# Where the residual's beta is added: a GpSimd addition moved from the scan stage to the coupling stage, with two swaps in ScalarE's order

## What is computed

```python
x = layernorm(x + coupling(x))                 # x2, the residual tokens of the next layer
xz = x @ w_in.T + b_in;  x_ssm, z = split(xz);  z = silu(z)
dt = softplus(x_ssm @ w_dt.T + b_dt)
Bm, Cm = x_ssm @ w_B.T + b_B, x_ssm @ w_C.T + b_C
h_n = exp(A_n * dt) * h_n + dt * Bm_n * x_ssm  # along the sequence, 16 states n
y = sum_n(h_n * Cm_n) + D * x_ssm
pre = (y * z) @ w_out.T + b_out + x            # residual: x is x2
attn = (pre - mean) * rsqrt(var + eps) * gamma + beta
x = layernorm(x + attn)                        # x2 + beta + gamma * normalized
```

## Time and profile before

| | |
|---|---|
| median of three runs | 1106.31 us (1105.72 to 1107.59) |
| the profiled execution: its own time | 1105.93 us |
| its span, first to last instruction | 1104.1 us |
| TensorE matmul busy | 991.2 us (90%) |
| VectorE busy | 935.2 us (85%) |
| ScalarE busy | 850.1 us (77%) |
| GpSimd busy | 720.8 us (65%) |
| DMA, mean share of 16 engines | 45.5% |
| mean granted TensorE clock | 0.970 |

### The profile page before, as it was taken

One profiled execution on the slowest core, in us unless ns is written; L12 is line 12 of the kernel. 1 busy time (PEld: TensorE's weight loads), 2 busy tenths in 40 slices (PEclk: granted clock), 3 DMA queues, 4 the chain that ended last, 5 costly groups with the idle time before them and its releaser, 6 DMA issues. The chain is left out here.

```text
span 1104.1 us, 17792 instructions
## 1 busy us (share of the span) xinstructions
PE 991.2 (90%) x5502; PEld 742.3 (67%) x5502; DVE 935.2 (85%) x1232; ACT 850.1 (77%) x1664; POOL 720.8 (65%) x623
## 2 busy tenths in 40 slices
PE   6999999999969999998758699999999999988887
PEld 4777777777755555555546477767777777777776
DVE  7999999999955888865889998999999999999851
ACT  7778878877646677777767798898988989887843
POOL 3466566756760112215878998989989898999630
PEclk9999999999998999999878899999999999999899
DMA  6444434443415001114967675456665558665201
GB/s 187 128 134 120 134 102 139 121 121 104 120 30 192 1 29 49 39 57 107 247 142 188 129 169 134 138 148 140 173 147 161 150 135 171 146 148 141 78 11 39
DMA packets 93249, 133.86 MB, mean 121 GB/s; under 512 B 8802, under 2 KB 47714, under 8 KB 93156
## 3 DMA queue, kind: packets, MB, share of 16 engines
q1 hardware_dynamic: 93156, 132.73, 45.5%
HBM read 116.45 MB, written 14.16 MB: 118 GB/s over the span
## 5 line engine op out<-in xcount | busy, mean ns | idle before, releaser
L2325 DVE TENSOR_TENSOR_SCAN ob<-bank_a,h,ob 128x512 f32<-128x512 f32 x128 | 159.7, 1269 | 15.6 <-ACT bank_a L1992 13.4
L2325 DVE TENSOR_TENSOR_SCAN oa<-bank_a,h,oa 128x512 f32<-128x512 f32 x128 | 160.5, 1271 | 12.7 <-ACT h L2001 6.7
L1804 PE MATMUL bank_m<-w,f_h 128*128 128x256 f32 x448 | 104.5, 383 | 0.0
L1481 POOL TENSOR_TENSOR oa<-ob,x1T 128x1024 f32<-128x1024 f32 x8 | 18.8, 2354 | 129.9 <-DVE ob L1381 129.9
L1992 ACT ACTIVATE bank_a<-s,A 128x512 f32<-128x512 f32 x128 | 86.6, 684 | 17.7 <-DVE ob L2325 13.6
L1992 ACT ACTIVATE bank_a<-dtc,A 128x512 f32<-128x512 f32 x128 | 86.7, 684 | 15.5 <-DVE ob L2325 10.0
L1804 PEld LDWEIGHTS bank_m<-w,f_h 128*128 128x128 f32 x448 | 84.7, 193 | 13.0 <-issue 2.4
L1749 PE MATMUL bank_y<-ident,ob 128*128 128x128 f32 x512 | 71.6, 286 | 19.2 <-POOL ob L2558 13.3
L883 POOL TENSOR_TENSOR xd<-xs,L 128x512 f32<-128x512 f32 x32 | 33.9, 1060 | 76.0 <-DVE xs L662 76.0
L1749 PEld LDWEIGHTS bank_y<-ident,ob 128*128 128x128 f32 x512 | 63.2, 148 | 29.6 <-POOL ob L2558 14.2
L673 DVE TENSOR_TENSOR_SCAN L<-abc,zeros,b_id 128x512 f32<-128x512 f32 x64 | 78.3, 1265 | 5.2 <-POOL xd L883 4.2
(11 more groups left out here) (407 smaller groups left out, 2944.3 us busy)
## 6 DMA issues: line engine op xcount, KB each, us to landing
Bb<-CB_rows SPq DMA_DIRECT2D x128, 256.0 KB, 5.2
Cb<-CB_rows SPq DMA_DIRECT2D x128, 256.0 KB, 4.9
abc<-decays SPq DMA_DIRECT2D x32, 512.0 KB, 4.4
Ebc<-ramps SPq DMA_DIRECT2D x64, 128.0 KB, 3.1
uT<-in_uT SPq DMA_DIRECT2D x8, 512.0 KB, 4.3
u<-in_u SPq DMA_DIRECT2D x8, 512.0 KB, 3.8
x_tokens<-x2s SPq DMA_DIRECT2D x8, 512.0 KB, 3.4
x_rows<-x1T SPq DMA_DIRECT2D x8, 512.0 KB, 2.9
```

The costliest lines, as they stand in the source:

```text
L1804: i = e.matmul(to, f_h[:, k, c * CH:(c + 1) * CH], w2[:, k, :], start=False, stop=(c % 2 == 1 and k == KF - 1))
L2325: e.tensor_tensor_scan(s[:, k, :], p_a[k][:, :], s[:, k, :], h0[:, n, k:k + 1], ALU.mult, ALU.add).then_inc(v_s, 1)
```

## The change

Beta is added to `x2s` by GpSimd in the coupling stage, for blocks 0 to 5 two iterations after the block's last normalization (behind `to_channels`, which still reads the tile without beta) and for blocks 6 and 7 in round 0 of the scan stage. `shifted`, `end_shifted` and their waits go. `residual` now reads x2 + beta, so beta is subtracted from the row of b_out once, by two VectorE operations on one partition each. The stores of `x2s` move behind the stores of the rows, and those of blocks 6 and 7 move into round 1, ahead of `load_x2`, which waits for them. On ScalarE the row of C of state 8 moves from before `soft_step` to behind the factors of state 9, whose first half moves ahead of `soft_step`; the row of C of state 4 moves ahead of the second factor of state 5. VectorE takes product 8 behind the scans of state 9.

```diff
+        def store_tokens(e, b):
+            e.wait_ge(c_sh, b + 1)
+            e.dma_start(x2_tokens[:, b * NC:(b + 1) * NC, :], x2s[b % 2][:, :, :]).then_inc(c_tok[b % 2], DMAS)
...
             def sync(e, early_loads):
                 for b in range(NB):
-                    e.wait_ge(c_n, 4 * b + 4)
-                    e.dma_start(x2_tokens[:, b * NC:(b + 1) * NC, :], x2s[b % 2][:, :, :]).then_inc(c_tok[b % 2], DMAS)
                     if b == NB - 3:
...
                     e.dma_start(x2_rows[:, :, tokens(b)], x1T[:, :, tokens(b)]).then_inc(c_row, DMAS)
+                    if b < NB - 2:
+                        store_tokens(e, b)
                     if b == NB - 2:
                         early_loads(e)
...
                     if w == 10:
                         e.tensor_scalar(bias_f[:, 2 * DM:3 * DM], bias_f[:, 2 * DM:3 * DM], 0.5, None, ALU.mult).then_inc(c_w, 1)
+                        for i in (0, 32):
+                            e.tensor_tensor(bias_f[i:i + 1, DM:2 * DM], bias_f[i:i + 1, DM:2 * DM], bet[i:i + 1, :], ALU.subtract).then_inc(c_w, 1)
...
+                def shift(b):
+                    e.wait_ge(c_bT, 2 * b + 2)
+                    e.sem_inc(step, 1)
+                    e.tensor_tensor(x2s[b % 2][:, :, :], x2s[b % 2][:, :, :], bet.rearrange("p (o f) -> p o f", o=1).to_broadcast([P, NC, DM]), ALU.add).then_inc(c_sh, 1)
...
                     if ended(w - 3) is not None:
                         norm(ended(w - 3))
+                    if ended(w - 6) is not None:
+                        shift(ended(w - 6))
                 drive()
...
             def sync(e):
+                    if post == 0:
+                        store_tokens(e, NB - 2)
+                        store_tokens(e, NB - 1)
                     if live(post):
                         load_x2(post)
...
             def scalar(e):
                     if live(post):
-                        spread_C(post, 8)
+                        decay(post, 9, 0)
                     if 0 < cur < NB:
                         soft_step(cur)
                     if live(post):
-                        decay(post, 9, 0)
                         decay(post, 9, 1)
+                        spread_C(post, 8)
                         carry(post, 8)
...
                         carry(cur, 4)
+                        spread_C(cur, 4)
                         decay(cur, 5, 1)
-                        spread_C(cur, 4)
...
             def vector(e):
                     if live(post):
-                        product(post, 8)
                         scan(post, 9, 0)
                         scan(post, 9, 1)
+                        product(post, 8)
...
             def pool(e):
-                def shifted(b):
-                    e.wait_ge(v_pre, 2 * b + 2)
-                    e.sem_inc(step, 1)
-                    e.tensor_tensor(x2, x2, rowwise(bet), ALU.add).then_inc(p_xb, 1)
...
                 def summed(b):
                     e.wait_ge(p_gam, b + 1)
-                    e.wait_ge(p_xb, b + 1)
+                    e.wait_ge(v_pre, 2 * b + 2)
...
                         into(cur, 5)
-                    if 0 <= post < NB - 1:
-                        shifted(post)
...
                     if 0 <= post < NB - 1:
                         summed(post)
+                    if cur == 0:
+                        c_shift(NB - 2)
                     if live(cur):
                         into(cur, 9)
                         into(cur, 10)
                     if 0 <= post < NB - 1:
                         norm45(post)
+                    if cur == 0:
+                        c_shift(NB - 1)
...
-                end_shifted(0)
                 end_root3(0)
                 end_root4(0)
                 end_root3(1)
-                end_shifted(1)
```

More of the change, by code:

```diff
@@ L1002, in build @@
         ld_B, ld_C = [d_sem(f"ld_B{i}") for i in range(4)], [d_sem(f"ld_C{i}") for i in range(4)]
+        c_sh = new_sem("c_sh")
         x2_tokens, x2_rows = scratch["x2_tokens"].rearrange("(n p) f -> p n f", p=P), rows(scratch["x2_rows"])
@@ L1185, in z_first @@
                 def z_first(p):
-                    e.wait_ge(c_w, 11)
+                    e.wait_ge(c_w, 13)
                     e.wait_ge(c_xT, 11 + p)
@@ L1443, in weights @@
                         e.tensor_scalar(bias_f[:, 2 * DM:3 * DM], bias_f[:, 2 * DM:3 * DM], 0.5, None, ALU.mult).then_inc(c_w, 1)
+                        for i in (0, 32):
+                            e.tensor_tensor(bias_f[i:i + 1, DM:2 * DM], bias_f[i:i + 1, DM:2 * DM], bet[i:i + 1, :], ALU.subtract).then_inc(c_w, 1)
                     if w == 11:
-                        e.wait_ge(c_w, 6)
+                        e.wait_ge(c_w, 8)
                         e.tensor_copy(bias[:, :], bias_f[:, :]).then_inc(c_w, 1)
@@ L1451, in weights @@
                     if w == 13:
-                        e.wait_ge(c_w, 7)
+                        e.wait_ge(c_w, 9)
                         e.tensor_tensor(bias[32:64, :], bias_f[32:64, :], bias[32:64, :].bitcast(F32), ALU.subtract).then_inc(c_w, 1)
@@ L1508, in pool @@
                         norm(ended(w - 3))
+                    if ended(w - 6) is not None:
+                        shift(ended(w - 6))
                 drive()
-                return norm
+                return norm, shift
             pc.close()
@@ L1549, in build @@
             v_s, v_g, v_gate, v_pre, v_l3, v_l4, v_l6, v_x3b = (d_sem("v_" + n) for n in ("s", "g", "gate", "pre", "l3", "l4", "l6", "x3b"))
-            p_b, p_l3, p_xb, p_gam, p_add, p_l4, p_l6 = (d_sem("p_" + n) for n in ("b", "l3", "xb", "gam", "add", "l4", "l6"))
+            p_b, p_l3, p_gam, p_add, p_l4, p_l6 = (d_sem("p_" + n) for n in ("b", "l3", "gam", "add", "l4", "l6"))
             ld_xT, ld_x2, st_o = (d_sem(n) for n in ("ld_xT", "ld_x2", "st_o"))
@@ L2397, in end_sum @@
                     e.wait_ge(v_m, 4 * p + 1)
-                    e.wait_ge(p_xb, Z + p + 1)
                     e.tensor_tensor(xl[:, half[p], :], xl[:, half[p], :], x2[:, half[p], :], ALU.add).then_inc(v_m, 1)
@@ L2640, in end_root @@
                     e.tensor_tensor(to, what, mhalf[:, 0:2], ALU.pow).then_inc(done, 1)
-                def end_shifted(p):
-                    e.wait_ge(v_pre, 2 * Z + p + 1)
-                    e.sem_inc(step, 1)
-                    e.tensor_tensor(x2[:, half[p], :], x2[:, half[p], :], row_wide(bet), ALU.add).then_inc(p_xb, 1)
                 def end_root3(p):
@@ L2657, in end_root6 @@
                     end_root(rs6[:, half[p]], ve6[:, half[p]], 7 + p, p_l6)
-                c_norm = c_pool(e)
+                c_norm, c_shift = c_pool(e)
                 into(0, 0)
```

## The result

| | before | after |
|---|---|---|
| median on one chip, 8 runs each | 1107.78 us | 1111.98 us |
| ratio of after to before, 95% interval | | 1.0041 (1.0028 to 1.0053) |
| profiled execution: its own time | 1105.93 us | 1111.8 us |
| its span | 1104.1 us | 1109.9 us |

The change makes the kernel slower by 4.2 us. I had forecast +0.65 (1107.0) in a range up to 1110.5, so the time lies outside the range and the sign I thought likeliest (no change) was wrong. It is the size of case C (+5), but not its mechanism.

The account below looks back on a forecast made before the run. The loop through Softplus was taken to set the round, with the loop through GpSimd's product almost as long. Terms -1.3 - 1.9 + 1.95 + 1.9 = +0.65 on 1106.31 gave about 1107.0 us, range 1102.0 to 1110.5 (8 in 10).

Parts of the forecast that it names:

- case C: Rival, coupling stage: four of five shifts delay VectorE's `low` by 1.6 each through the shared port; +5, 1111.5 us; chance 0.16.
- Inside coupling: Coupling stage: GpSimd's additions hold up VectorE's two-SBUF-input operations, second shift +1.6, first +0.3, others 0; together +1.9 us.
- From coupling to scan: Start of the scan stage: the sixth shift, between block 6's `norm` and `drive`, delays the first scan by +1.95 us.
- DMA: Round 1: stores of blocks 6 and 7 delay loads; state 3's `into` 3 to 4 us later, taken back by `scaled`: 0.
- Round 1: Scan stage, round 1: VectorE's shorter wait for state 9's factor comes through whole, -1.3 us.
- What is late next: Rounds 2 to 7: Softplus loop frees 1.3 a round, but the loop through GpSimd's product 14 leaves -1.9 us over six.
- The wait in front of: GpSimd ahead of `scaled`: without `shifted` its wait for ScalarE grows from 1.15 to 3.5 us and frees nothing by itself.

Follow-up runs that it names:

- stores_later: Changed kernel with the late stores of blocks 6 and 7 and `load_x2` behind the rows of C of state 1 and B of state 3: ratio 1.0041 to before.
- order_only: Kernel before with only the order swaps on ScalarE and VectorE, beta staying in the scan stage: ratio 0.9996 to before.
- both_swaps: Kernel before plus the swaps, TensorE's projection of B and C first, GpSimd's products 12 and 14 earlier: ratio 0.9943 to before, 1102.29 us.
- p14_swaps: Kernel before plus the swaps, TensorE's projection of B and C first, and GpSimd's product 14 alone earlier: ratio 0.9982 to before.
- sixth_ahead: Changed kernel with block 5's addition of beta in front of block 6's `norm` on GpSimd, not between it and `drive`: ratio 1.0020 to before.
- all_thin: Changed kernel with all eight additions of beta cut to 128 x 2, waits and stores kept: ratio 0.9996 to before.

## Why the prediction was wrong

- *Inside coupling*, +1.9: right, +1.5. It is the second addition alone, on `twist`, as named; the 0.3 for the first was 0.
- *From coupling to scan*, +1.95: right, +2.17. The addition took 2.75 there, not 2.37. Together 3.7 against 3.85.
- *DMA*, 0: right. The load was 3.92 us late and covered (`stores_later`).
- *Round 1*, -1.3: **the step that failed.** I wrote that the gain at state 9 comes through whole, because I followed GpSimd only. TensorE adds up product 8 ahead of projecting B and C, and I had not looked who stands behind the product that I let come later. From state 8 to state 12 the changed kernel gained 0.8 of the 1.3, `order_only` 0.0, and C to D came out 0.3 longer, not 1.3 shorter. In round 2, for which I had counted a gain as well, the same queue cost 0.6.
- *TensorE's clock*, for which my sum had no term: **the other failure, and the larger one.** In the changed kernel three projections ran at a lower granted clock than in the kernel before. They are worth 1.2 in round 0 (ahead of state 8), 1.1 in D to E and 0.6 in E to F, 2.9 in all. Both traces of the changed kernel have them. They don't go with beta's move: the first is as slow in `both_swaps` and the third nearly so in `p14_swaps` (3.23 us), which leave beta where it was, and none of the three is in `sixth_ahead`, `stores_later` or `all_thin`, whose schedules differ from the changed kernel's by little. Why all three fall in this kernel stays open, and the 2.9 is read from the traces: no run held the clock while all else stayed.
- *What is late next*, -1.9: the third failed term. The loop was the right one, the round of 66.0 too, but it gave 0.65 to 0.8 in five rounds, 0.15 each. The swaps do free 1.1 us a round at state 9. The free time in front of TensorE (0.3) is not the gain: from the product's end to the gate it takes 2.13 instead of 2.29 to 2.36, and product 12 in the same loop became a wait of 0.6. The last round, in which I counted a gain as well, gave 0.7 back (121.1 beside 120.4; the second trace of before has 121.3, so this part is not certain).
- *The wait in front of* `scaled`, 3.5: it is 2.05 to 2.26 in rounds 2 to 6 (1.13 to 1.77 before). GpSimd waits longer for other things ahead of it, in round 5 for instance 1.85 for a row of B where it had waited 0.83. The conclusion, that this time frees nothing, held.
- Sum by the first trace of each: +3.65 from A to C; +0.3 in C to D (+1.2 for the clock, -0.8 by state 12, -0.1 behind it); +2.35 in D to F (+1.1 and +0.6 for the clock, +0.6 for the queue); -0.8 in F to G and +0.7 behind it = +6.2, and -0.35 ahead of A: 5.85, the +5.8 between the spans. By the medians +4.2, as before's profiled execution was a short one.

So beta's move cost what I said, the swaps gave about 1.1 ahead of the last round where I had 3.2, and the clock cost 2.9. Rival C had the size by four port hits; there was one, so that its number is near is luck.

## What to carry to other kernels

When an operation is put later, list who waits for it on every engine and what is queued behind each of those waits, not only on the engine whose stall is to go. Free time at one joint of the next loop is not what removing the first loop gives: look for all joints of that loop (here two products), and change both loops before judging either. An addition that "only fills idle time" of one engine costs nearly its full length where it stands in front of a stage's first operation (2.2 of 2.75 us here), and holds up its neighbour where that reads two operands from SBUF (3.44 us beside 1.29). And compare the same matmuls in both traces before a difference is put down to the edit: here their clock made 2.9 of the 5.8 us between the two traces.

## What the runs showed of the hardware

TensorE's granted clock decides stretches of 1 us in rounds 0, 1 and 2 and in the last. Below is the windows view over one group of matmuls at a time, in the kernel before and in the changed one (PEclk is the third number from the right; 0.50 is 1.2 GHz, 1.00 is 2.4 GHz, and a value between them is a stretch with both). First four matmuls of 128x512 of the x projection in round 0:

```profile
534.61:537.05 2.44, 2.44 (x8) 1.21 (x7) 1.69 (x2) 1.98 (x3) 1.43 (x1) 0.77 0.99 236
```

```profile
537.92:541.54 3.62, 3.62 (x7) 1.55 (x6) 2.50 (x2) 1.97 (x3) 3.62 (x3) 0.50 0.97 162
```

The eight matmuls of the z projection in round 1:

```profile
587.24:589.13 1.89, 1.89 (x11) 1.63 (x10) 1.85 (x3) 0.00 (x0) 1.89 (x1) 1.00 0.92 170
```

```profile
590.99:593.86 2.87, 2.87 (x11) 2.37 (x10) 2.87 (x4) 0.00 (x0) 0.29 (x1) 0.66 0.90 161
```

Four matmuls of the projection to step sizes, later in the same round:

```profile
609.17:611.15 1.98, 1.98 (x6) 0.97 (x7) 1.98 (x3) 1.44 (x4) 1.98 (x2) 1.00 0.93 140
```

```profile
614.33:618.11 3.78, 3.78 (x5) 1.61 (x6) 3.78 (x5) 1.82 (x4) 3.78 (x3) 0.50 0.93 163
```

TensorE had been idle 3.06 us before and 2.86 us after ahead of the sums of product 14 that come before the z projection, so about the same wait goes with both outcomes. In each case ScalarE waits for the group or for what stands behind it on TensorE: its evacuation comes 1.2 later in round 0 (a wait of 1.75 instead of 0.57), `evac_gated` 1.1 later (D to E), and in E to F, where it waits 1.79, state 8 begins 0.6 later. In the last round the first group of eight behind a 2.7 us wait of TensorE took 1.89 us in five of the nineteen traces and 2.86 to 3.62 in the other fourteen. The changed kernel had the same outcome in both of its traces at all four places, the kernel before at the first three (2.44 and 2.76, 1.89 and 1.89, 1.98 and 1.98 us) and not in the last round (1.89 and 2.94). A gain of under 1 us in this kernel can be lost at such a place, and can't be read from the whole time.
